# Linear attention block of a perceiver layer: the output weight is multiplied into the per-head key-value matrices, and q is divided before it is transposed

## The reference

```python
qkv = x @ W_qkv
q, k, v = jnp.split(qkv, 3, axis=-1)
q = rmsnorm(q, qn_w)
k = rmsnorm(k, kn_w)
...
q = jax.nn.relu(q)
k = jax.nn.relu(k)
kv = jnp.einsum('bhnd,bhne->bhde', k, v)
out = jnp.einsum('bhnd,bhde->bhne', q, kv)
k_sum = k.sum(axis=2)
normalizer = jnp.einsum('bhnd,bhd->bhn', q, k_sum) + EPS_DEN
out = out / normalizer[..., None]
...
return out @ W_out + b_out
```

## Time and profile before

| | |
|---|---|
| median of 3 runs | 545.12 us (544.13 to 545.36) |
| profiled execution, its time | 544.86 us |
| profiled execution, its span | 543.1 us |
| PE busy | 535.8 us, 99% of the span |
| DVE busy | 347.3 us, 64% |
| POOL busy | 200.6 us, 37% |
| stage of the linear attention | about 410 to 470 us |

### The profile page before, as it was taken

How to read it: one execution, slowest core, us unless ns; L and a number is a source line. 1 busy time by engine, 2 the same in 40 slices (tenths; PEclk the granted TensorE clock), 3 DMA queues, 4 the chain that set the end, 5 groups by cost and what they waited for, 6 DMA issues and landing times.

```text
span 543.1 us, 6839 instructions
## 1 busy us (share of the span) xinstructions
PE 535.8 (99%) x2498; PEld 444.2 (82%) x2498; DVE 347.3 (64%) x564; ACT 255.6 (47%) x416; POOL 200.6 (37%) x132
## 2 busy tenths in 40 slices
PE   8999999999999999999999999999999999999997
PEld 7788888788888888888888888888887888888886
DVE  5574455685566866566799654799665327638757
ACT  4743334764544544444545444557356452561210
POOL 4625050323111322243145522447336959800000
PEclk9999999999999999999999999999999999999999
DMA  8711222242322223423222221243420314200002
GB/s 313 289 53 58 84 103 91 79 154 78 141 93 77 78 88 145 155 79 112 91 107 78 79 78 39 77 157 116 147 86 1 111 45 127 107 1 1 0 1 77
DMA packets 14864, 51.59 MB, mean 95 GB/s; under 512 B 1776, under 2 KB 1776, under 8 KB 14192
## 3 DMA queue, kind: packets, MB, share of 16 engines
q1 hardware_dynamic: 14832, 51.16, 26.3%
HBM read 50.11 MB, written 1.05 MB: 94 GB/s over the span
## 4 chain that ended last, share of the span: by engine, by line
PE 93%; ACT 1%; POOL 1%; issue 1%; DVE 1%; DMA 1%; SPq 0%; DVEq 0%; POOLq 0%
PE bank L1241 26%; PE bank L1322 11%; PE bank L1324 11%; PE bank L1323 11%; PE bank L1311 10%; PE bank L1313 10%; PE bank L1312 10%; PE bank L1231 1%; POOL w_v_l L485 1%; DMA wo_raw<-wo_t 1%; PE bank L1469 1%; PE bank L1478 0%; PE bank L1350 0%; PE bank L1597 0%; PE bank L1431 0%
## 5 line engine op out<-in xcount | busy, mean ns | idle before, releaser
L499 POOL TENSOR_TENSOR cn_l<-raw_n,cn_h 128x1024 fp32r<-128x1024 f32 x32 | 80.1, 2502 | 201.8 <-ACT cn_h L645 201.8
L932 DVE TENSOR_TENSOR top<-top,bank 128x512 f32<-128x512 f32 x60 | 41.3, 688 | 98.6 <-ACT ring L663 98.4
L1311 PE MATMUL bank<-qk_h,ct_h 128*128 128x512 f32 x256 | 100.5, 393 | 1.1 <-DVE top L932 1.1
L1322 PE MATMUL bank<-ph,cn_h 128*128 128x512 f32 x256 | 100.3, 392 | 0.0
L1313 PE MATMUL bank<-qk_h,ct_l 128*128 128x512 f32 x256 | 99.7, 390 | 0.0
L1324 PE MATMUL bank<-ph,cn_l 128*128 128x512 f32 x256 | 99.7, 389 | 0.0
L1323 PE MATMUL bank<-pl,cn_h 128*128 128x512 f32 x256 | 99.6, 389 | 0.0
L1312 PE MATMUL bank<-qk_l,ct_h 128*128 128x512 f32 x256 | 99.6, 389 | 0.0
L663 ACT COPY ring<-bank 128x512 f32<-128x512 f32 x64 | 37.6, 587 | 73.3 <-PE bank L1313 73.3
L670 ACT ACTIVATE ph<-ring 128x512 fp32r<-128x512 f32 x64 | 40.5, 633 | 66.2 <-PE bank L1324 44.5
L962 DVE TENSOR_TENSOR ring<-ring,shift_b 128x512 f32<-128x512 f32 x64 | 62.6, 983 | 1.9 <-ACT shift_b L681 1.9
(11 more groups left out here) (219 smaller groups left out, 863.0 us busy)
## 6 DMA issues: line engine op xcount, KB each, us to landing
raw_t<-ctx_t SPq DMA_DIRECT2D x32, 512.0 KB, 4.1
raw_n<-ctx_n SPq DMA_DIRECT2D x32, 512.0 KB, 3.3
piece_raw<-pieces SPq DMA_DIRECT2D x12, 512.0 KB, 3.2
wv_raw<-wv_in SPq DMA_DIRECT2D x4, 256.0 KB, 4.6
wo_raw<-wo_t SPq DMA_DIRECT2D x4, 256.0 KB, 4.9
xs<-x SPq DMA_DIRECT2D x4, 256.0 KB, 4.8
wq_raw<-wq_t SPq DMA_DIRECT2D x4, 256.0 KB, 5.9
wk_raw<-wk_in SPq DMA_DIRECT2D x1, 1024.0 KB, 7.6
```

Source lines behind the costliest of these rows:

```text
L499: pool.tensor_tensor(cn[p % CNB][1][:], raw_n[p % 2][:], cn[p % CNB][0][:].bitcast(F32), ALU.subtract).then_inc(cnl_ready, 1)
L932: dve.tensor_tensor(top[n % 2][:], top[n % 2][:], bank[:, S_BANKS[i % 2], :], ALU.max).then_inc(max_done, 1)
L1311: pe.matmul(bank[:, dst, :], ct[i // 2 % 2][0][:, c, keys], qk[0][:, c, :], start=(c == 0), stop=False)
L1322: pe.matmul(bank[:, c, :], keys[0][:, q % 2, d], ph[q % PB][:], start=first, stop=False)
```

## The change

- PE projects in the order k0, k1, q0, k2, k3, q1, q2, q3, v0, v1, v2, v3 (`PROJECTIONS`), so v comes last.
- The sum of the keys over the tokens is made by POOL (`k_sum`, three additions of 128x512) and by one matmul with ones, which puts it on every partition (`KSUM_BANK`).
- DVE multiplies q by its norm weights (`weigh_q`), and for each tile (`normalise_q`) multiplies by the key sums, sums over each head, adds the epsilon term (a tensor_scalar of 128x16 in SBUF), takes the reciprocal, and multiplies relu(q) by it. These quotients, and no longer the heads, are transposed and split.
- PE makes the key-value matrix transposed (values x keys, 128x128). DVE masks it into SBUF (`kv_full`), ACT rounds it (`high_kv`), DVE subtracts (`low_kv`), PE multiplies it by the output weight (KVW, four times three matmuls of 128x512), ACT and DVE split that (`high_kvw`, `low_kvw`), and z is the product of the quotients with it.
- `linear`, `transpose_q` of the raw q, `qrT` with its ACT work and the four columns of ones are gone.
- POOL splits the output weight ahead of v's, and the pieces of the experts in another rhythm; `w_v`'s high parts move on ACT behind the layer norm.

```diff
+PROJECTIONS = (("k", 0), ("k", 1), ("q", 0), ("k", 2), ("k", 3), ("q", 1), ("q", 2), ("q", 3), ("v", 0), ("v", 1), ("v", 2),
+               ("v", 3))
+SQUARES = [(kind, t) for kind, t in PROJECTIONS if kind != "v"]
...
-            pool.wait_ge(y_psum, TT)
-            pool.memset(vs[:, :, :, P:VW], 1.0).then_inc(pads_ready, 1)
...
-            pool.wait_ge(y_psum, TT)
-            for n in range(0, 4):
+            pool.wait_ge(k_ready, 2)
+            pool.tensor_tensor(k_sum[:], ks[:, 0, :], ks[:, 1, :], ALU.add).then_inc(k_sum_step, 1)
+            split_piece(0)
+            for t in range(2, TT):
+                pool.wait_ge(k_ready, t + 1)
+                pool.wait_ge(k_sum_step, t - 1)
+                pool.tensor_tensor(k_sum[:], k_sum[:], ks[:, t, :], ALU.add).then_inc(k_sum_step, 1)
+            for n in range(1, 3):
                 split_piece(n)
             pool.wait_ge(xn_ready, 2 * TT)
             for t in range(TT):
                 pool.tensor_tensor(xs[:, t, :], xs[:, t, :], row("b_out"), ALU.add).then_inc(bout_added, 1)
+            split_piece(3)
             pool.wait_ge(v2_psum, TT)
-            for n in range(4, 8):
+            for n in range(4, 10):
                 split_piece(n)
...
+            high_w2("v", 0)
+            square_of("k", 0)
+            high_xT(2 * TT + 2, X1_BANKS)
+            root("k", 0)
+            high_w2("v", 1)
+            square_of("k", 1)
+            high_xT(2 * TT + 3, X1_BANKS)
+            root("k", 1)
+            for kind, t in SQUARES[2:]:
+                square_of(kind, t)
+                root(kind, t)
+            copy_v(0)
+            copy_v(1)
+            high_xT(3 * TT, QN_BANKS)
+            copy_v(2)
+            high_xT(3 * TT + 1, QN_BANKS)
+            copy_v(3)
+            high_xT(3 * TT + 2, QN_BANKS)
+            high_kv(0)
+            high_kv(1)
+            high_xT(3 * TT + 3, QN_BANKS)
+            high_kv(2)
+            high_kv(3)
+            for c in range(C):
+                high_kvw(c)
...
+            def weigh_q(t):
+                dve.wait_ge(q_ssq, SQUARES.index(("q", t)) + 1)
+                dve.tensor_scalar(rms[:, t, 1:2], ssq[:, t, 1:2], DEN_EPS * DEN_EPS / D, DEN_EPS * DEN_EPS * RMS_EPS, ALU.mult,
+                                  ALU.add).then_inc(ms_ready, 1)
+                if t == 0:
+                    dve.wait_ge(qn_row_loaded, 16)
+                dve.tensor_tensor(qs[:, t, :], bank[:, KQV_BANKS[PROJECTIONS.index(("q", t)) % 6], :], qn_row[:],
+                                  ALU.mult).then_inc(qw_ready, 1)
+            def normalise_q(t):
+                dve.wait_ge(qw_ready, t + 1)
+                dve.wait_ge(ksumb_psum, 1)
+                wait(dve, q_k_summed, t)
+                dve.scalar_tensor_tensor(out=q_k[:], in0=qs[:, t, :], scalar=0.0, in1=bank[:, KSUM_BANK, :], op0=ALU.max,
+                                         op1=ALU.mult).then_inc(q_k_ready, 1)
+                dve.wait_ge(q_k_ready, t + 1)
+                dve.reduce_sum(norm[:, t, :], q_k[:].rearrange("p (h e) -> p h e", e=DH), AX.X).then_inc(q_k_summed, 1)
+                dve.wait_ge(q_k_summed, t + 1)
+                dve.wait_ge(rms_ready, SQUARES.index(("q", t)) + 1)
+                dve.tensor_scalar(norm[:, t, :], norm[:, t, :], rms[:, t, 1:2], None, ALU.add).then_inc(norm_ready, 1)
+                dve.wait_ge(norm_ready, t + 1)
+                dve.reciprocal(rnorm[:, t, :], norm[:, t, :]).then_inc(rnorm_ready, 1)
+                dve.wait_ge(rnorm_ready, t + 1)
+                heads = qs[:, t, :].rearrange("p (h e) -> p h e", e=DH)
+                dve.scalar_tensor_tensor(out=heads, in0=heads, scalar=0.0,
+                                         in1=rnorm[:, t, :].unsqueeze(2).to_broadcast([P, C * HG, DH]), op0=ALU.max,
+                                         op1=ALU.mult).then_inc(qn_ready, 1)
...
+            def mask_kv(c):
+                if c == 0:
+                    dve.wait_ge(masks_ready, MASKS)
+                dve.wait_ge(kv_psum, c + 1)
+                dve.tensor_tensor(kv_full[:, c, :], bank[:, KV_BANKS[c], 0:P], kvmask[:], ALU.mult).then_inc(kvf_ready, 1)
+            def low_kv(c):
+                dve.wait_ge(kvh_ready, c + 1)
+                dve.tensor_tensor(kv_t[1][:, c, :], kv_full[:, c, :], kv_t[0][:, c, :].bitcast(F32),
+                                  ALU.subtract).then_inc(kvl_ready, 1)
+            k_of(0)
+            low_xT(2 * TT + 2, X1_BANKS)
+            k_of(1)
+            low_xT(2 * TT + 3, X1_BANKS)
+            weigh_q(0)
+            k_of(2)
+            k_of(3)
+            for t in range(1, TT):
+                weigh_q(t)
+            normalise_q(0)
+            normalise_q(1)
+            low_xT(3 * TT, QN_BANKS)
+            normalise_q(2)
+            low_xT(3 * TT + 1, QN_BANKS)
+            normalise_q(3)
+            low_xT(3 * TT + 2, QN_BANKS)
+            mask_kv(0)
+            mask_kv(1)
+            low_kv(0)
+            low_kv(1)
+            mask_kv(2)
+            low_xT(3 * TT + 3, QN_BANKS)
+            mask_kv(3)
+            low_kv(2)
+            low_kv(3)
             for c in range(C):
-                dve.wait_ge(kv_psum, c + 1)
-                dve.tensor_tensor(kv[:, c, :], bank[:, KV_BANKS[c], 0:VW], kvmask[:], ALU.mult).then_inc(kv_ready, 1)
-            for t in range(TT):
-                dve.wait_ge(la_psum, t + 1)
-                la = bank[:, LA_BANKS[t]:LA_BANKS[t] + 2, 0:2 * VW].rearrange("p b (g w) -> p b g w", g=2)
-                dve.tensor_scalar(norm[:, t].rearrange("p (b g) h -> p b g h", b=2), la[:, :, :, P:VW], DEN_EPS, None,
-                                  ALU.add).then_inc(norm_ready, 1)
-                dve.wait_ge(norm_ready, t + 1)
-                dve.reciprocal(rnorm[:, t], norm[:, t]).then_inc(rnorm_ready, 1)
-                dve.wait_ge(rnorm_ready, t + 1)
-                for b in range(2):
-                    ins = dve.tensor_tensor(
-                        heads[:, t, b * 2 * P:(b + 1) * 2 * P].rearrange("p (g h e) -> p g h e", g=2, h=HG),
-                        la[:, b, :, 0:P].rearrange("p g (h e) -> p g h e", h=HG),
-                        rnorm[:, t, 2 * b:2 * b + 2, :].unsqueeze(3).to_broadcast([P, 2, HG, DH]), ALU.mult)
-                ins.then_inc(heads_ready, 1)
...
+                dve.wait_ge(kvwh_ready, c + 1)
+                dve.tensor_tensor(kvw[1][:, c, :], bank[:, KVW_BANKS[c], :], kvw[0][:, c, :].bitcast(F32),
+                                  ALU.subtract).then_inc(kvwl_ready, 1)
...
+            def key_value(c):
                 for t in range(TT):
-                    ins = pe.matmul(bank[:, KV_BANKS[c], 0:VW], ks[:, t, c * P:(c + 1) * P], vs[:, t, c, :],
+                    ins = pe.matmul(bank[:, KV_BANKS[c], 0:P], vs[:, t, c * P:(c + 1) * P], ks[:, t, c * P:(c + 1) * P],
                                     start=(t == 0), stop=(t == TT - 1))
                 ins.then_inc(kv_psum, 1)
...
+            pe.wait_ge(k2_ready, 2)
+            projection(0)
+            transpose_x1(2)
+            projection(1)
+            transpose_x1(3)
+            pe.wait_ge(w2_ready, 2)
+            for n in range(2, 7):
+                projection(n)
+            pe.wait_ge(k_sum_step, TT - 1)
+            pe.wait_ge(xl_ready, 2 * TT + 3)
+            pe.matmul(bank[:, KSUM_BANK, :], ones[:].to_broadcast([P, P]), k_sum[:], start=True,
+                      stop=True).then_inc(ksumb_psum, 1)
+            projection(7)
+            pe.wait_ge(w2_ready, 2 * len(W2_ORDER))
+            projection(8)
+            projection(9)
+            transpose_q(0)
+            projection(10)
+            transpose_q(1)
+            projection(11)
+            transpose_q(2)
+            pe.wait_ge(k_ready, TT)
+            pe.wait_ge(v_ready, TT)
+            key_value(0)
+            key_value(1)
+            transpose_q(3)
+            key_value(2)
+            key_value(3)
+            for c in range(C):
+                pe.wait_ge(kvl_ready, c + 1)
+                pe.wait_ge(xl_ready, 3 * TT + c + 1)
+                project(KVW_BANKS[c], [cut(kv_t, c, 0, P)], [cut(wout, c, 0, D)]).then_inc(kvw_psum, 1)
...
-                project(HEAD_BANKS[t], [cut(xT, c, t * P, (t + 1) * P) for c in range(C)],
-                        [cut(wout, c, 0, D) for c in range(C)]).then_inc(z_psum, 1)
-                if t < 2:
-                    transpose_heads(t + 2)
+                for c in range(C):
+                    if t == 0:
+                        pe.wait_ge(kvwl_ready, c + 1)
+                    ins = project(Z_BANKS[t], [cut(xT, c, t * P, (t + 1) * P)], [cut(kvw, c, 0, D)], starts=(c == 0),
+                                  stops=(c == C - 1))
+                ins.then_inc(z_psum, 1)
```

223 lines of the change are left out of this document (85 added, 138 removed).

## The result

The changed kernel takes 551.2 us (median of 4 runs, 550.34 to 552.93), the kernel before 544.79 beside it (544.13 to 545.36). The ratio is 1.012, its 95% interval 1.0107 to 1.0132: slower by 6.4 us. Forecast were 550.4, range 545.2 to 553.2. The profiled execution is one of the longer ones: 552.03 us, with a span of 550.1.

A forecast was written before the change was run, and what follows sets the result against it. PE, busy 99% of the span, was taken as the bound. Work -1.9, old waits -1.2 and new waits, mostly DVE held up by POOL, summed to +5.0; with +0.5 for the small tensor_scalar, 544.86 + 5.5 = 550.4 us, range 545.2 to 553.2.

The forecast's parts named there:

- PE's work: Matmuls and transposes removed (5.46 us) against products added (3.58 us) on PE: -1.9 us.
- the removed waits: PE's old waits before v0, z0 and the second x2 transpose disappear: together 1.2 us saved.
- without any other effect: Sum of PE's work, removed waits and 2.5 us of added waits, with DVE not held up: -0.6 us.
- (a): k1, now the second projection, waits for tile 1's split: PE idle 1.5 us.
- (b): The key-value product waits for v3's copy, now covered by only one group of transposes: 0.44 us.
- (c): The second x2 transpose, between the z products, waits for its layer norm: 0.5 us.
- The eight instructions: Four divisions and four low parts on DVE, both inputs in SBUF, wait for POOL; the whole sum becomes +5.0 us.
- the walk: Stage followed instruction by instruction on the old kernel's clock, giving PE's waits and z3 later by 5.0 us.
- The 128x16 tensor_scalar: DVE's small SBUF instruction may wait for POOL: +0 to +2.9 us, taken +0.5; walked through, stage 5.5 to 7.9 later.
- Rival 1: Only the divisions or only the low parts are held up: +1.0 to +1.1 us, 545.9 us; chance 0.14.
- Rival 4: Granted clock falls in 447 to 461 us, some 4 us of matmuls at half speed: 554 to 556 us; chance 0.04.
- POOL's pieces: POOL ends its weight pieces some 5 us later, but they are used more than 20 us later: no cost.

The follow-up runs named there:

- e4: The changed kernel with the head sums, reciprocals and full key-value matrix kept in PSUM instead of SBUF; 545.07 us, ratio 0.999 to 1.0011.
- e1: The changed kernel with POOL's b_out additions and its pieces from the fourth on held until DVE's last low part is done; 547.64 us.
- e5: The changed kernel with only the head sums in PSUM, so the 128x16 tensor_scalar reads PSUM; 550.91 us, ratio 1.0068 to 1.012.
- e10: The changed kernel with head sums and full key-value matrix in PSUM, leaving only the divisions with two SBUF inputs; 546.4 us.
- e9: The changed kernel with unread matmuls on PE, 10 before the fourth transpose of q and 6 before the third output-weight product; 550.57 us.
- e3: The changed kernel with head sums and reciprocals in PSUM, so only the low parts still have two SBUF inputs; 546.32 us.
- e8: As e1, but with POOL's memset of the convolution's pads ahead of piece 6 instead of behind piece 9; 547.36 us.
- e2: The changed kernel with the full key-value matrix in PSUM, so the low parts read only one input from SBUF; 549.31 us.

## Why the prediction was right

**PE's work and the removed waits, -1.9 - 1.2.** With nothing on DVE held up (e4, e1), the stage is 0.44 us shorter than before; forecast was 0.6. The sum "without any other effect" is shown as a whole; the parts of PE's work were not measured one by one.

**(a) k1 waits for tile 1's split, 1.5 us.** Right: k1 starts at 415.88 - 0.48 = 415.40, forecast 415.4. The 1.32 in the row's brackets is the same wait, counted from the transposes' modelled end. But it isn't what undoing it gives: 0.57, since the tile is late for k1 in the next place too.

**(b) v3's copy, 0.44, and (c) the second x2 transpose, 0.5.** In brackets these are 0.33 us in e4 (0.24 in the changed kernel) and 0.28. The forecast counted them from start to start, 0.44 us after a group of four transposes begins. So counted, e4 has 449.24 - 448.31 - 0.44 = 0.49 and 465.13 - 464.24 - 0.44 = 0.45. Both were right within 0.1 us, and what lies between the -0.44 and the -0.6 is not in the waits; where it is was not tried.

**The eight instructions wait for POOL: +5.0 on the sum.** Shown by e4 and e1. The rule that an instruction behind another loses to a POOL instruction that already waits was right too, in the pairs of low parts. Seven of them waited; for the third division, which the walk had late by 0.7, POOL was idle. PE's waits came out differently at two places. Before the fourth transpose PE waits 2.33 us by the bracket, 2.5 from start to start (forecast 1.7), because the small tensor_scalar is held up too: without it, in e5 and e10, the bracket has 1.35. Before the first product with the output weight it then waits 0.16 us (456.38 - 454.51 = 1.87 against e4's 1.71; forecast 1.2), as PE itself is later. The small wait stands before the second transpose (0.22) and not the third (0.3). The other three products were right: from start to start they are 1.05, 2.45 and, at the upper clock in e9, 1.04 us apart, forecast 1.05, 2.5 and 1.1. The last low part ends at 460.87 - 0.48 = 460.4, forecast 460.0. At the upper clock this date sets the rest (in e9 the fourth product starts at 461.01, behind its low part's end at 460.95), and so the sum held although two parts were off in opposite directions. The walk's +5.0, or +5.5 with the small instruction, stands against 63.40 - 58.05 = 5.35 in e9's stage.

**The 128x16 tensor_scalar, +0 to +2.9, taken +0.5.** It does wait: two of the four take 1.07 and 1.79 us, against 0.23 when the input is in PSUM. The Trainium skill (VectorE: DVE Perf Modes, Mode 2×_2P) has a tensor_scalar from SBUF to SBUF use both of DVE's read ports, and none with a source in PSUM; these rows agree, in that only the one from SBUF waits for POOL. What it costs is another thing. In the changed kernel the low parts' dates swallow nearly all (e5: 0.3 us by the medians, not told from nothing). The mechanism was right. The +0.5 was picked near the low end of a wide range and not worked out, so that it is about the size is luck. The 5.5 to 7.9 us of the walk with it start just above what was measured (6.46 in the profiled stage, the clock's fall included, 5.35 without it in e9), but not by that walk's rows: PE was to wait 0.9 before the first transpose and 2.0 before the second, and waits 0 and 0.22.

**Rival 1, one kind held up: +1.0 to +1.1 each.** Measured in the stages of e3 and e10, 1.1 both; by the medians 1.3 and 1.1. That the two together cost about five times that was the walk's main statement, and it was right.

**Rival 4, the clock: the step that failed.** I gave it 0.04, "it stays at 1.00 in the rows, though none has so loose a stretch", with some 4 us of matmuls at half speed. It does fall, in a part of the executions, the profiled one among them, for eight matmuls. Its chance was too low and its size too large. In the sum it stood at nothing, and it is what the sum lacks: the changed kernel is 6.4 us above the kernel before beside it, e9 is 5.3 above its own, forecast was 5.5. The four runs of the changed kernel are too few to say how much of a median the fall makes up.

**POOL's pieces, "some 5 us later, which they use more than 20 us later".** Right in what follows for the changed kernel, whose PE is busy for all of 480 to 520 us; the pieces end at 482.55 - 0.48 = 482.1 instead of 475.5, 6.6 us later. e1 shows how far that reaches: with the pieces until 492.6 us it is no longer so, and not through the pieces themselves but through DVE, which POOL then meets in the router.

## What to carry to other kernels

Before new work goes to DVE, look at what POOL does at that time and count the new instruction's inputs in SBUF: the same division or subtraction with one operand left in PSUM cost nothing here, and the twelve instructions that read SBUF alone cost 6 us together. Costs of such waits don't add: two kinds that lengthened the stage by 1.6 us each made some 6 together (e5 against e4, less the clock's 1.1), because the first used up the slack that hid the second and moved it under other instructions of POOL, and taking out a third kind gave nothing that could be measured. When a wait is mended by moving POOL's work, follow that work to its new place, its small instructions as well, before counting the gain.

## What the runs showed of the hardware

- A tensor_scalar of 128x16 fp32 within SBUF, 0.23 us of work at most, waits for a POOL instruction's end as the wide ones do (up to 1.79 us), and so do comparisons of 128x64 (2.43 us instead of 0.21, e8). The tensor_reduce of 128x512 from SBUF between them never took more than 0.69.
- POOL pays as well: its subtraction takes 2.71 and 2.68 us where it meets such a DVE instruction, 2.35 to 2.40 otherwise, and its four additions 5.51 instead of 5.03 in e3 and e4, where the divisions read their second input from PSUM.
- After an idle 2.3 us and a second one of 1.5, PE ran eight matmuls at the lower clock (0.43 us apart instead of 0.227) in the profiled execution, and by the runs' mean clocks not in all of them; in e2 it fell right after the first 2.32 us. With sixteen matmuls whose results nobody reads (e9) the profile shows 1.00 there and all six runs a mean of 1.0.
